# Expert slots of a mixture-of-experts layer: the moved x goes through a stage buffer to a dense matmul operand

## The chip, the core and the metric

The kernel runs on one core of a Trainium2 chip. Its time is the device time of one launch in microseconds (us); lower is better. Three runs of the kernel before gave a median of 1057.66 us, from 1057.39 to 1059.92.

## The reference

The kernel computes one transformer layer on x of shape 8 x 256 x 512 (2048 tokens of 512 floats), all in float32: cross attention to a context, then a mixture of experts. Only the second half matters here, with `h` the layer norm of the attention's result:

```python
logits = h @ gate_w.T                      # 32 experts
rw = softmax(logits); sel = top_k(sigmoid(logits), 4)
w = rw[sel] / rw[sel].sum()
cw_large[t, sel] += w                      # 32 large experts, inner width 192
cw_small[t, sel // 2] += w                 # 16 small experts, inner width 128
a = silu(h @ Wg[e]) * (h @ Wu[e]) * cw[:, e]
large = sum over e of a @ Wd[e]            # the same for small with cWg, cWu, cWd
x = x + large + 0.05 * small
```

## The kernel before, in words

Three stages follow one another, each a block of five instruction streams with a barrier between: `attention` (to 403 us), `route` (403 to 455 us) and `experts` (455 us to the end). Only the last has to do with most of the change.

`route` writes the normed tokens and the 32 weights of each to `xd` in DRAM, 544 floats a row (XW), and sorts the 8192 pairs of token and expert into slots of 128 tokens of one expert. There are at most 96 slots (NS); with these inputs 78 are run. Tables in SBUF tell of each slot: the token numbers (`tok`), the rows of the result (`dst`), the expert (`slot_e`) and which of four weight buffers it is in (`slot_buf`). A large expert and its small one are computed side by side, 192 + 128 = 320 columns (IW).

In `experts`, slot s uses buffers of parity p = s % 2, and its work goes through five queues:

- GpSimd, `gather(s)`: copies a column of `tok` to `idx`, and an indirect DMA brings the 128 rows to `xg`. `add(s)` adds the slot's y to the result by an indirect DMA that accumulates; each waits for the one before it.
- VectorE, `turn(s)`: transposes xg in blocks of 32 x 32 to `xb`, with a written step of four floats.
- ScalarE, `x_move(s)`: four DMAs move the 32-row quarters of xb so that each lands on all 128 partitions of `xT`. After all four, xT is x transposed, laid out [128, 128 tokens, 4]: the weight operand `xT[p][:, :, c]` of L1633 has a step of four floats.
- TensorE, `gate_up(s)`: 4 + 4 products of 128 x 128 with 320 columns, to `g_ps` and `u_ps`. In the profile each float32 product is two matmuls, so 8 and 8.
- ScalarE `silu(s)`, then VectorE `gated(s)`: a = silu(g) * u * the slot's weight column `wt`, which `weights_of` takes from xg by the expert's number.
- TensorE `transpose_a(s)` (three turns of a), VectorE `at_evac(s)` to `aT`, TensorE `down(s)`: 3 products (6 matmuls) of 512 columns to `y_ps`, ScalarE `y_evac(s)` to `yb`.

The order within a turn of the loop is written out by hand for each engine. For slot s: TensorE does transpose_a(s-1), gate_up(s), down(s-1). ScalarE does silu(s), x_move(s+2), y_evac(s-1). VectorE does at_evac(s-1), turn(s+2), gated(s), weights_of(s+2). GpSimd does add(s-1), gather(s+4). SyncE loads the next expert's weights into one of four buffers as slots are done. Slots 0 and 1 stand before the loop; a register loop over pairs of slots follows, with an `If` that skips the unused pairs up to NS. Each engine handles its instructions in order.

Of the kernel before, what the change touches and what calls it, by code (L numbers as in the profile page):

```python
# [5 lines left out]
ALU = mybir.AluOpType  # L6
ACT = mybir.ActivationFunctionType
AX = mybir.AxisListType
F32 = mybir.dt.float32
I32 = mybir.dt.int32  # L10
# [4 lines left out]
P = 128  # L15
# [972 lines left out]
def route(nc, gw, gw_loaded, xs, ident, new, xd, out, tabs, wts, W, w_loaded, kept, xd_stored):  # L988
# [5 lines left out]
    with ExitStack() as ctx:  # L994
# [130 lines left out]
        def _(act):  # L1125
# [42 lines left out]
            act.preload_act_table_set("natural_log_exp_and_others")  # L1168
# [135 lines left out]
        def _(dve):  # L1304
# [55 lines left out]
            dve.memset(tok[:, NS:NS + 4], 0)  # L1360
            dve.memset(slot_e[:, NS:NS + 4], 0)
            dve.memset(slot_buf[:, NS:NS + 4], 0)
# [64 lines left out]
def experts(nc, ident, xd, out, tabs, wts, W, w_loaded):  # L1427
# [4 lines left out]
    with ExitStack() as ctx:  # L1432
# [6 lines left out]
        xg = [sb(f"xg{i}", [P, XW], F32) for i in range(2)]  # L1439
        wt = [sb(f"wt{i}", [P, 2], F32) for i in range(2)]  # L1440
        xb = [sb(f"xb{i}", [P, D], F32) for i in range(2)]
        xT = [sb(f"xT{i}", [P, P, C], F32) for i in range(2)]
# [4 lines left out]

        g_ps = [ps(f"g_ps{i}", [P, 512]) for i in range(2)]
# [5 lines left out]
        turned, gu_full = sem("turned"), sem("gu_full")  # L1454
        x_ready = [sem(f"x_ready{i}") for i in range(2)]
        wt_ready = sem("wt_ready")
# [6 lines left out]
        def moved(s, p):  # L1463

            return (s - p) * (QB * DMA // 2) + QB * DMA
# [25 lines left out]
        @block.gpsimd  # L1491
        def _(pool):
            def gather(s, p):

                if not (isinstance(s, int) and s < 2):
                    pool.wait_ge(turned, s - 1)
                    pool.wait_ge(wt_ready, s - 1)
                pool.tensor_copy(idx[p][:, :], tok[:, bass.ds(s, 1)]).then_inc(idx_ready, 1)  # L1498
                pool.wait_ge(idx_ready, s + 1)
                pool.sem_inc(passed, 1)  # L1500
                pool.indirect_dma_start(xg[p][:, :], None, xd[:, :], bass.IndirectOffsetOnAxis(idx[p][:, :], 0))\  # L1501
                    .then_inc(x_loaded[p], DMA)

            def add(s, p):


                pool.tensor_copy(yidx[p][:, :], dst[:, bass.ds(s, 1)]).then_inc(yi_ready, 1)
                pool.wait_ge(yi_ready, s + 1)
                pool.sem_inc(passed, 1)
                pool.wait_ge(y_empty, s + 1)  # L1510
                pool.sem_inc(passed, 1)
                if not (isinstance(s, int) and s == 0):
                    pool.wait_ge(y_added, s * DMA)
                    pool.sem_inc(passed, 1)
                pool.indirect_dma_start(out[:, :], bass.IndirectOffsetOnAxis(yidx[p][:, :], 0), yb[p][:, :], None,  # L1515
                                        compute_op=ALU.add).then_inc(y_added, DMA)

            for s in range(4):
                gather(s, s % 2)
            gather(4, 0)  # L1520
            add(0, 0)
            gather(5, 1)
            n, last = count(pool)
            with pool.Fori(1, NS // 2) as i:
                with pool.If(i < n):
                    for p in range(2):
                        add(i * 2 + p - 1, 1 - p)
                        gather(i * 2 + p + 4, p)
            add(last + 1, 1)
            pool.wait_ge(y_added, last * DMA + 2 * DMA)  # L1530
            for p in range(2):
                pool.wait_ge(x_loaded[p], n * DMA + 2 * DMA)

        @block.scalar
        def _(act):
            def x_move(s, p):

                act.wait_ge(turned, s + 1)
                if not (isinstance(s, int) and s < 2):
                    act.wait_ge(gu_full, s - 1)  # L1540
                for i in range(QB):
                    act.dma_start(xT[p][:, i * Q:(i + 1) * Q, :].rearrange("m r c -> m (r c)"),  # L1542
                                  xb[p][i * Q:(i + 1) * Q, :]).then_inc(x_ready[p], DMA)
# [11 lines left out]
            def slot(s, p, first=False):  # L1555
                silu(s, p)
                x_move(s + 2, p)
                if not first:
                    y_evac(s - 1, 1 - p)

            x_move(0, 0)
            x_move(1, 1)
            slot(0, 0, first=True)
# [12 lines left out]
        def _(dve):  # L1576
# [4 lines left out]
            def weights_of(s, p):  # L1581

                e = dve.value_load(slot_e[0:1, bass.ds(s, 1)], min_val=0, max_val=E_ - 1)  # L1583
                dve.wait_ge(x_loaded[p], (s - p) * (DMA // 2) + DMA)
                if not (isinstance(s, int) and s < 2):
                    dve.wait_ge(a_ready, s - 1)
                dve.tensor_copy(wt[p][:, 0:1], xg[p][:, bass.ds(e + D, 1)]).then_inc(wt_ready, 1)
                dve.wait_ge(wt_ready, s + 1)
                dve.tensor_scalar(wt[p][:, 1:2], wt[p][:, 0:1], SMALL, None, ALU.mult)

            def turn(s, p):

                dve.wait_ge(x_loaded[p], (s - p) * (DMA // 2) + DMA)
                if not (isinstance(s, int) and s < 2):
                    dve.wait_ge(x_ready[p], moved(s - 2, p))
                dve.transpose(xb[p][:, :].rearrange("p (j r c) -> p j c r", r=Q, c=C), xg[p][:, 0:D]).then_inc(turned, 1)  # L1596
# [10 lines left out]
            for p in range(2):  # L1607
                turn(p, p)
                weights_of(p, p)
            turn(2, 0)  # L1610
            gated(0, 0)
            weights_of(2, 0)
            at_evac(0, 0)
            turn(3, 1)
            gated(1, 1)
            weights_of(3, 1)
            n, last = count(dve)
            with dve.Fori(1, NS // 2) as i:  # L1618
                with dve.If(i < n):  # L1619
                    for p in range(2):  # L1620
                        at_evac(i * 2 + p - 1, 1 - p)
                        turn(i * 2 + p + 2, p)
                        gated(i * 2 + p, p)
                        weights_of(i * 2 + p + 2, p)
# [3 lines left out]
        def _(pe):  # L1628
            def gate_up(s, p, buf):
                pe.wait_ge(x_ready[p], moved(s, p))  # L1630
                for ps_, g in ((g_ps, 0), (u_ps, 1)):
                    for c in range(C):
                        m = pe.matmul(ps_[p][:, 0:IW], xT[p][:, :, c],  # L1633
                                      W[:, bass.ds(buf, 1), (2 * c + g) * IW:(2 * c + g + 1) * IW]
                                      .rearrange("p a f -> p (a f)"),
                                      start=(c == 0), stop=(c == C - 1))
                m.then_inc(gu_full, 1)
# [26 lines left out]

            slot(0, 0, first=True)
# [6 lines left out]
            transpose_a(last + 1, 1)  # L1672
            down(last + 1, 1, pe.value_load(slot_buf[0:1, bass.ds(last + 1, 1)], min_val=0, max_val=NW - 1))


def build(nc, t, out):
    xd = nc.dram_tensor("xd", (NT * P, XW), F32, kind="Internal").ap()
    with ExitStack() as ctx:
# [6 lines left out]
        tabs = (sb("tok", [P, NS + 4], U32), sb("dst", [P, NS], U32), sb("slot_e", [P, NS + 4], I32),  # L1685
                sb("slot_buf", [P, NS + 4], I32), sb("cum_i", [P, E_], I32), sb("turns", [P, 2], I32))
# [50 lines left out]
```

## Time and profile before

| | |
|---|---|
| median of three runs | 1057.66 us |
| the profiled execution | 1061.51 us, its span 1059.8 us |
| TensorE busy | 986.3 us, 93% |
| VectorE, ScalarE, GpSimd busy | 49%, 30%, 28% |
| mean granted TensorE clock | 0.965 |
| HBM traffic | 123 GB/s over the span |

A row of a timeline gives the start in us from the span's beginning, the length in us, the engine, the line, the operation and its tiles, and in brackets the idle time before it and what ended it. PE is TensorE's matmul, PEld its weight load, DVE VectorE, ACT ScalarE, POOL GpSimd; a q behind a name means the queue of that engine, as for the issue of a DMA. Matmuls overlap, so the distance between starts is their cost, not their length.

### The profile page before, as it was taken

How to read it: one execution, taken by the hardware profiler on the slowest of the kernel's cores; microseconds unless marked ns; L12 is line 12 of the kernel's file. 1: busy time of each engine (PE TensorE's matmuls, PEld its weight loads, DVE VectorE, ACT ScalarE, POOL GpSimd, SP SyncE). 2: the span in 40 equal slices, each digit the busy share in tenths (PEclk: the TensorE clock that was granted, in tenths of full speed). 3: DMA queues.
4: the chain of work that ended last, by engine and by line, in shares of the span. 5: the costliest groups of instructions: out<-in, count | busy, mean ns of one | idle time of the engine just before them, and what ended most of it. 6: DMA issues, size and time to landing. Idle time of an engine off the chain costs nothing.

```text
span 1059.8 us, 18705 instructions
## 1 busy us (share of the span) xinstructions
PE 986.3 (93%) x5163; PEld 726.0 (69%) x5164; DVE 524.5 (49%) x1233; ACT 314.0 (30%) x631; POOL 300.3 (28%) x399
## 2 busy tenths in 40 slices
PE   7789999999999988449999999999999999999994
PEld 6557666676665535337878778777787777877872
DVE  4677677777677726933333333333333333333331
ACT  2245465555555535901111111111111111111110
POOL 3011101011120001223434344343443434434432
PEclk9999999999999989669999999999999999999997
DMA  6163234231431008227897998989888899889563
GB/s 208 45 166 77 66 91 102 86 86 56 121 80 51 32 31 304 105 72 174 219 244 181 249 253 219 243 218 254 199 221 215 211 259 249 213 208 251 111 114 68
DMA packets 102603, 168.23 MB, mean 159 GB/s; under 512 B 15520, under 2 KB 65824, under 8 KB 98208
## 3 DMA queue, kind: packets, MB, share of 16 engines
q1 hardware_dynamic: 36624, 103.11, 31.0%
q0 software_dynamic: 17792, 43.30, 21.6%
q10 hardware_dynamic: 48144, 21.25, 7.4%
q8 instruction: 27, 0.44, 0.2%
q14 instruction: 16, 0.13, 0.0%
HBM read 101.29 MB, written 29.36 MB: 123 GB/s over the span
## 4 chain that ended last, share of the span: by engine, by line
PE 54%; DMA 1%; issue 1%; DVEq 0%; DVE 0%; ACTq 0%; POOL 0%; ACT 0%; SPq 0%; POOLq 0%
PE y_ps L1650 19%; PE g_ps L1633 17%; PE u_ps L1633 16%; PE at_ps L1642 2%; DMA xg<-xd,gidx 0%; DMA xT<-xb 0%; ACTq L1542 0%; POOL out_x L1515 0%; DVEq L1618 0%; DVE xb L1596 0%; ACT sg L1547 0%; DVEq L1583 0%; ACT yb L1553 0%; DVE aT L1579 0%; DVEq L1619 0%
## 5 line engine op out<-in xcount | busy, mean ns | idle before, releaser
L1650 PE MATMUL y_ps<-W,aT 128*128 x468 | 216.3, 598 | 3.6 <-DVE aT L1579 3.6
L1633 PE MATMUL g_ps<-W,xT 128*128 x624 | 192.2, 451 | 13.3 <-DMA xT<-xb 13.0
L1515 POOL DMA_INDIRECT out_x<-yb,yidx x78 | 125.3, 1606 | 278.1 <-ACT yb L1553 194.4
L518 DVE TENSOR_REDUCE mx<-s 128x2 f32<-128x512 f32 x256 | 163.4, 682 | 59.3 <-PE s L709 58.6
L397 ACT ACTIVATE pt<-stp 128x512 f32<-128x512 f32 x256 | 139.1, 596 | 148.1 <-PE stp L723 147.4
L1633 PE MATMUL u_ps<-W,xT 128*128 x624 | 180.7, 432 | 0.0
L1633 PEld LDWEIGHTS g_ps<-W,xT 128*128 128x128 f32 x624 | 168.3, 311 | 15.2 <-issue 15.1
L1633 PEld LDWEIGHTS u_ps<-W,xT 128*128 128x128 f32 x624 | 171.0, 308 | 0.0
L1650 PEld LDWEIGHTS y_ps<-W,aT 128*128 128x128 f32 x468 | 89.6, 192 | 85.7 <-issue 79.6
L1596 DVE STREAM_TRANSPOSE xb<-xg 128x512 f32<-128x512 f32 x80 | 89.1, 1114 | 79.5 <-DMA xg<-xd,gidx 76.2
L1547 ACT ACTIVATE sg<-g_ps 128x320 f32<-128x320 f32 x78 | 34.2, 438 | 305.8 <-PE u_ps L1633 305.8
L1600 DVE SCALAR_TENSOR_TENSOR a<-u_ps,wt,sg 128x192 f32<-128x192 f32 x78 | 32.6, 418 | 183.8 <-ACT sg L1547 183.8
L1553 ACT COPY yb<-y_ps 128x512 f32<-128x512 f32 x78 | 45.7, 586 | 197.5 <-PE y_ps L1650 116.0
L1501 POOL DMA_INDIRECT xg<-xd,gidx x82 | 82.7, 1008 | 65.4 <-POOL gidx L1498 64.6
L709 PE MATMUL s<-kst,qst 96*128 96x256 bf16 x512 | 81.7, 275 | 10.5 <-DVE mx L518 9.8
L1579 DVE COPY aT<-at_ps 128x384 f32<-128x384 f32 x78 | 43.5, 558 | 87.9 <-PE at_ps L1642 82.9
L723 PE MATMUL stp<-qst,kst 98*128 98x256 bf16 x512 | 78.3, 276 | 4.0 <-DMA qst<-nm 4.0
L709 PEld LDWEIGHTS s<-kst,qst 96*128 96x128 bf16 x512 | 44.1, 98 | 51.2 <-DVE mx L518 24.1
L739 PE MATMUL ov<-pt,vx 128*32 128x256 f32 x1024 | 70.0, 392 | 1.9 <-ACT xo L381 1.8
L1498 POOL COPY gidx<-tok 128x1 uint32 (+1 forms) x82 | 60.0, 732 | 28.2 <-POOLq L994 17.2
L767 PE MATMUL side<-Wfc,oT 128*128 128x512 f32 x128 | 62.1, 601 | 1.5 <-ACT oT L387 1.5
L723 PEld LDWEIGHTS stp<-qst,kst 98*128 98x128 bf16 x512 | 49.5, 98 | 17.9 <-issue 5.6
(197 smaller groups left out, 842.9 us busy)
## 6 DMA issues: line engine op xcount, KB each, us to landing
W<-in_wts SPq DMA_DIRECT2D x32, 1280.0 KB
W<-in_wts SPq DMA_DIRECT2D x32, 768.0 KB
xT<-xb ACTq DMA_DIRECT2D x320, 64.0 KB
qst<-q SPq DMA_DIRECT2D x42, 256.0 KB, 5.0
xs<-in_x SPq DMA_DIRECT2D x8, 512.0 KB, 3.6
ctxT<-in_ctx SPq DMA_DIRECT2D x8, 512.0 KB, 4.0
out_x<-xs SPq DMA_DIRECT2D x16, 256.0 KB, 2.3
kst<-k SPq DMA_DIRECT2D x48, 64.0 KB, 2.1
```

The source lines that it names most:

```text
L397: act.activation(pt[g % 2][:, 2 * (j % 2) + r, :, :], stp[n % STP][:, :, :], ACT.Exp, scale=DH ** -0.5).then_inc(exp_done, 1)
L518: dve.tensor_reduce(mx[j // CH % 2][:, h:2 * G:G], s1[r][:, :, :], AX.X, ALU.max)\
L709: m = pe.matmul(s1[r][:, t, :], qst[b % 2][0:ROWS_QK, head(j, r), t * P:(t + 1) * P], kst[b % 2][0:ROWS_QK, head(j, r) // C, :], start=Tru ...
L723: m = pe.matmul(stp[n % STP][:, t, :], kst[b % 2][0:ROWS_ST, head(j, r) // C, t * P:(t + 1) * P], qst[b % 2][0:ROWS_ST, head(j, r), :], st ...
L739: m = pe.matmul(ov[c * VW:(c + 1) * VW, g % 2, :], vx[b % 2][:, t, g % 2 * C + c, :], pt[(b * G + g) % 2][:, c, t, :], start=(t == 0), sto ...
L767: m = pe.matmul(side[:, :], oT[t][:, c, :], Wfc[:, c, :], start=(c == 0), stop=(c == C - 1))
L1498: pool.tensor_copy(idx[p][:, :], tok[:, bass.ds(s, 1)]).then_inc(idx_ready, 1)
L1501: pool.indirect_dma_start(xg[p][:, :], None, xd[:, :], bass.IndirectOffsetOnAxis(idx[p][:, :], 0))\
L1515: pool.indirect_dma_start(out[:, :], bass.IndirectOffsetOnAxis(yidx[p][:, :], 0), yb[p][:, :], None, compute_op=ALU.add).then_inc(y_added, ...
L1596: dve.transpose(xb[p][:, :].rearrange("p (j r c) -> p j c r", r=Q, c=C), xg[p][:, 0:D]).then_inc(turned, 1)
L1633: m = pe.matmul(ps_[p][:, 0:IW], xT[p][:, :, c], W[:, bass.ds(buf, 1), (2 * c + g) * IW:(2 * c + g + 1) * IW] .rearrange("p a f -> p (a f) ...
L1650: m = pe.matmul(y_ps[:, :], aT[p][:, c, :], W[:, bass.ds(buf, 1), GW + c * D:GW + (c + 1) * D].rearrange("p a d -> p (a d)"), start=(c == ...
```

## The change

For slots from 1 on, the moved x lands in a new `stage` buffer, laid out [128, quarter, chunk, 32], and VectorE's new `place(s)` copies it to xT, which is now [128, chunk, 128 tokens]: the operand of a product is dense. The turn reads with a step of four floats and writes with none; the rows of the gate and up weights are ordered on the host to fit. The turn and the move run three slots ahead instead of two, the gather five instead of four. The weight column is taken in two steps: `weight_next` (to `wn`, with the turn) and `weight_now` (to `wt`).

The orders become: ScalarE x_move(s+3), silu(s), y_evac(s-1); VectorE at_evac(s-1), weight_now(s+1), place(s+1), turn(s+3), gated(s); GpSimd add(s-1), gather(s+5). TensorE's order stays.

Slot 0's x is transposed by TensorE from xg to `xt_ps` and copied to xT by ScalarE. Sixteen identity transposes run on TensorE ahead of it and sixteen ahead of the last down. The first four gathers index `tok` directly. `route` loses one preload of an activation table, and the tables get six spare columns instead of four.

```diff
-            act.preload_act_table_set("natural_log_exp_and_others")
...
-            dve.memset(tok[:, NS:NS + 4], 0)
-            dve.memset(slot_e[:, NS:NS + 4], 0)
-            dve.memset(slot_buf[:, NS:NS + 4], 0)
+            dve.memset(tok[:, NS:NS + 6], 0)
+            dve.memset(slot_e[:, NS:NS + 6], 0)
+            dve.memset(slot_buf[:, NS:NS + 6], 0)
...
+        wn = [sb(f"wn{i}", [P, 1], F32) for i in range(2)]
...
-        xT = [sb(f"xT{i}", [P, P, C], F32) for i in range(2)]
+        stage = [sb(f"stage{i}", [P, QB, C, Q], F32) for i in range(2)]
+        xT = [sb(f"xT{i}", [P, C, P], F32) for i in range(2)]
...
+        xt_ps = ps("xt_ps", [P, 512])
...
-        turned, gu_full = sem("turned"), sem("gu_full")
+        xt_full, x0_ready, turned, copied, gu_full = (sem(n) for n in ("xt_full2", "x0_ready", "turned", "copied",
+                                                                       "gu_full"))
...
-        wt_ready = sem("wt_ready")
+        wn_ready, wt_ready = sem("wn_ready"), sem("wt_ready")
...
-            return (s - p) * (QB * DMA // 2) + QB * DMA
+            return (s - p) * (QB * DMA // 2) + p * QB * DMA
...
             def gather(s, p):
...
+                if isinstance(s, int) and s == 2:
+                    pool.wait_ge(xt_full, 1)
+                elif not (isinstance(s, int) and s < 2):
+                    pool.wait_ge(turned, s - 2)
...
-                    pool.wait_ge(turned, s - 1)
-                    pool.wait_ge(wt_ready, s - 1)
-                pool.tensor_copy(idx[p][:, :], tok[:, bass.ds(s, 1)]).then_inc(idx_ready, 1)
-                pool.wait_ge(idx_ready, s + 1)
-                pool.sem_inc(passed, 1)
-                pool.indirect_dma_start(xg[p][:, :], None, xd[:, :], bass.IndirectOffsetOnAxis(idx[p][:, :], 0))\
+                    pool.wait_ge(wn_ready, s - 1)
+                if isinstance(s, int) and s < 4:
+                    rows = tok[:, s:s + 1]
+                else:
+                    pool.tensor_copy(idx[p][:, :], tok[:, bass.ds(s, 1)]).then_inc(idx_ready, 1)
+                    pool.wait_ge(idx_ready, s - 3)
+                    pool.sem_inc(passed, 1)
+                    rows = idx[p][:, :]
+                pool.indirect_dma_start(xg[p][:, :], None, xd[:, :], bass.IndirectOffsetOnAxis(rows, 0))\
...
             def add(s, p):
...
-            for s in range(4):
+            for s in range(6):
...
-            gather(4, 0)
...
-            gather(5, 1)
+            gather(6, 0)
...
                 with pool.If(i < n):
...
-                        gather(i * 2 + p + 4, p)
+                        gather(i * 2 + p + 5, 1 - p)
...
-                pool.wait_ge(x_loaded[p], n * DMA + 2 * DMA)
+                pool.wait_ge(x_loaded[p], n * DMA + (3 - p) * DMA)
...
             def x_move(s, p):
...
-                act.wait_ge(turned, s + 1)
-                if not (isinstance(s, int) and s < 2):
-                    act.wait_ge(gu_full, s - 1)
+                act.wait_ge(turned, s)
+                if not (isinstance(s, int) and s < 3):
+                    act.wait_ge(copied, s - 2)
...
-                    act.dma_start(xT[p][:, i * Q:(i + 1) * Q, :].rearrange("m r c -> m (r c)"),
+                    act.dma_start(stage[p][:, i, :, :].rearrange("m c r -> m (c r)"),
...
             def slot(s, p, first=False):
+                x_move(s + 3, 1 - p)
...
-                x_move(s + 2, p)
...
-            x_move(0, 0)
+            act.wait_ge(xt_full, 1)
+            act.copy(xT[0][:, :, :], xt_ps[:, :].rearrange("p (c t) -> p c t", c=C)).then_inc(x0_ready, 1)
             x_move(1, 1)
+            x_move(2, 0)
...
-            def weights_of(s, p):
+            def weight_next(s, p):
...
+                dve.tensor_copy(wn[p][:, :], xg[p][:, bass.ds(e + D, 1)]).then_inc(wn_ready, 1)
+            def weight_now(s, p):
+                dve.wait_ge(wn_ready, s + 1)
...
-                dve.tensor_copy(wt[p][:, 0:1], xg[p][:, bass.ds(e + D, 1)]).then_inc(wt_ready, 1)
+                dve.tensor_copy(wt[p][:, 0:1], wn[p][:, :])
+                dve.tensor_scalar(wt[p][:, 1:2], wn[p][:, :], SMALL, None, ALU.mult).then_inc(wt_ready, 1)
...
-                dve.tensor_scalar(wt[p][:, 1:2], wt[p][:, 0:1], SMALL, None, ALU.mult)
...
             def turn(s, p):
...
-                dve.wait_ge(x_loaded[p], (s - p) * (DMA // 2) + DMA)
+                weight_next(s, p)
+                if not (isinstance(s, int) and s < 3):
+                    dve.wait_ge(x_ready[p], moved(s - 2, p))
+                dve.transpose(xb[p][:, :], xg[p][:, 0:D].rearrange("t (c q j) -> t j c q", c=C, j=QB)).then_inc(turned, 1)
+            def place(s, p):
+                dve.wait_ge(x_ready[p], moved(s, p))
...
-                    dve.wait_ge(x_ready[p], moved(s - 2, p))
-                dve.transpose(xb[p][:, :].rearrange("p (j r c) -> p j c r", r=Q, c=C), xg[p][:, 0:D]).then_inc(turned, 1)
+                    dve.wait_ge(gu_full, s - 1)
+                dve.tensor_copy(xT[p][:, :, :].rearrange("m c (i r) -> m c i r", i=QB),
+                                stage[p][:, :, :, :].rearrange("m i c r -> m c i r")).then_inc(copied, 1)
...
             def gated(s, p):
...
-            for p in range(2):
-                turn(p, p)
-                weights_of(p, p)
+            weight_next(0, 0)
+            weight_now(0, 0)
+            turn(1, 1)
...
-            gated(0, 0)
-            weights_of(2, 0)
-            at_evac(0, 0)
-            turn(3, 1)
-            gated(1, 1)
-            weights_of(3, 1)
+            def slot(s, p, first=False):
+                if not first:
+                    at_evac(s - 1, 1 - p)
+                weight_now(s + 1, 1 - p)
+                place(s + 1, 1 - p)
+                turn(s + 3, 1 - p)
+                gated(s, p)
+            slot(0, 0, first=True)
+            slot(1, 1)
...
-                        at_evac(i * 2 + p - 1, 1 - p)
-                        turn(i * 2 + p + 2, p)
-                        gated(i * 2 + p, p)
-                        weights_of(i * 2 + p + 2, p)
+                        slot(i * 2 + p, p)
...
+            def transpose_x0():
+                pe.wait_ge(x_loaded[0], DMA)
+                for c in range(C):
+                    m = pe.transpose(xt_ps[:, c * P:(c + 1) * P], xg[0][:, c * P:(c + 1) * P], ident[:, :])
+                m.then_inc(xt_full, 1)
+            def keep_clock(n):
+                for _ in range(n):
+                    pe.transpose(xt_ps[:, 0:P], ident[:, :], ident[:, :])
             def gate_up(s, p, buf):
-                pe.wait_ge(x_ready[p], moved(s, p))
+                if isinstance(s, int) and s == 0:
+                    pe.wait_ge(x0_ready, 1)
+                else:
+                    pe.wait_ge(copied, s)
...
-                        m = pe.matmul(ps_[p][:, 0:IW], xT[p][:, :, c],
+                        m = pe.matmul(ps_[p][:, 0:IW], xT[p][:, c, :],
...
+            keep_clock(16)
+            transpose_x0()
...
+            keep_clock(16)
...
-        tabs = (sb("tok", [P, NS + 4], U32), sb("dst", [P, NS], U32), sb("slot_e", [P, NS + 4], I32),
-                sb("slot_buf", [P, NS + 4], I32), sb("cum_i", [P, E_], I32), sb("turns", [P, 2], I32))
+        tabs = (sb("tok", [P, NS + 6], U32), sb("dst", [P, NS], U32), sb("slot_e", [P, NS + 6], I32),
+                sb("slot_buf", [P, NS + 6], I32), sb("cum_i", [P, E_], I32), sb("turns", [P, 2], I32))
...
-        gu = np.stack([both("g"), both("u")], 2).reshape(E_, QB, C, Q, 2, IW).transpose(0, 3, 1, 2, 4, 5)
-        gu = gu.reshape(E_, P, GW)
+        gu = np.stack([both("g"), both("u")], 2).reshape(E_, C, P, 2, IW).transpose(0, 2, 1, 3, 4).reshape(E_, P, GW)
```

## Rows read from the trace of the kernel before

**Rows 1.** The page, part 4: shares of the span in the chain of waits, by line.
```profile
PE y_ps L1650 19%; PE g_ps L1633 17%; PE u_ps L1633 16%; PE at_ps L1642 2%; DMA xg<-xd,gidx 0%; DMA xT<-xb 0%; ACTq L1542 0%; POOL out_x L1515 0%; DVEq L1618 0%; DVE xb L1596 0%; ACT sg L1547 0%; DVEq L1583 0%; ACT yb L1553 0%; DVE aT L1579 0%; DVEq L1619 0%
```

**Rows 2.** Timeline of slot 32: start us, length us, engine, line, operation, tiles, [idle before].
```profile
701.90 0.49 PE L1642 MATMUL at_ps<-ident,a 128*128 128x128 f32 x3
...
702.23 2.44 PE L1633 MATMUL g_ps<-W,xT 128*128 x8
...
702.43 0.56 DVE L1579 COPY aT<-at_ps 128x384 f32<-128x384 f32 x1 [1.18 <-PE at_ps L1642]
...
704.32 1.11 DVE L1596 STREAM_TRANSPOSE xb<-xg 128x512 f32<-128x512 f32 x1 [1.34 <-DMA xg<-xd,gidx]
704.50 2.32 PE L1633 MATMUL u_ps<-W,xT 128*128 x8
...
706.65 2.74 PE L1650 MATMUL y_ps<-W,aT 128*128 x6
...
706.85 0.44 ACT L1547 ACTIVATE sg<-g_ps 128x320 f32<-128x320 f32 x1 [3.72 <-PE u_ps L1633]
706.99 2.52 ACTq L1542 DMA_DIRECT2D xT<-xb  x4
...
707.66 0.34 DVE L1602 SCALAR_TENSOR_TENSOR a<-u_ps,wt,sg 128x128 f32<-128x128 f32 x1
...
709.23 0.49 PE L1642 MATMUL at_ps<-ident,a 128*128 128x128 f32 x3
...
709.63 0.59 ACT L1553 COPY yb<-y_ps 128x512 f32<-128x512 f32 x1 [2.34 <-PE y_ps L1650]
```

**Rows 3.** Groups by form (busy us, mean ns | idle), two single lines (ns min/median/max).
```profile
L1633 PEld LDWEIGHTS g_ps<-W,xT 128*128 128x128 f32 x624 | 168.3, 311 | 15.2 <-issue 15.1
...
L1650 PEld LDWEIGHTS y_ps<-W,aT 128*128 128x128 f32 x468 | 89.6, 192 | 85.7 <-issue 79.6
L1596 DVE STREAM_TRANSPOSE xb<-xg 128x512 f32<-128x512 f32 x80 | 89.1, 1114 | 79.5 <-DMA xg<-xd,gidx 76.2 <-DMA xT<-xb 3.0
...
L1587 DVE COPY wt<-xg 128x1 f32 x80 | 12.3, 154 | 25.7 <-DVE a L1602 25.7
...
L1542 ACTq DMA_DIRECT2D xT<-xb x320: 550/626/1295, 461.4 to 1039.3; - x160
...
L1369 DVE TENSOR_SCALAR xl<-xs,mv_new,rstd_new x5: 543/545/548, 406.5 to 408.3; 128x512 f32<-128x512 f32 x5
```

**Rows 4.** Timeline of VectorE: three turns that waited for the gathered x.
```profile
498.54 1.11 DVE L1596 STREAM_TRANSPOSE xb<-xg 128x512 f32<-128x512 f32 x1 [1.18 <-DMA xg<-xd,gidx]
...
889.62 1.11 DVE L1596 STREAM_TRANSPOSE xb<-xg 128x512 f32<-128x512 f32 x1 [2.84 <-DMA xg<-xd,gidx]
...
1027.16 1.11 DVE L1596 STREAM_TRANSPOSE xb<-xg 128x512 f32<-128x512 f32 x1 [1.11 <-DMA xg<-xd,gidx]
```

**Rows 5.** Timeline of the expert stage's start; one window's busy times, clock, DMA.
```profile
460.31 1.08 DVE L1596 STREAM_TRANSPOSE xb<-xg 128x512 f32<-128x512 f32 x1 [4.60 <-DMA xg<-xd,gidx]
...
461.42 5.27 ACTq L1542 DMA_DIRECT2D xT<-xb  x8
...
466.64 4.17 PE L1633 MATMUL g_ps<-W,xT 128*128 x8 [12.97 <-DMA xT<-xb]
...
474.21 0.55 PE L1642 MATMUL at_ps<-ident,a 128*128 128x128 f32 x3 [1.24 <-DVE a L1602]
...
469.00:470.00 1.00, 1.00 (x3) 0.63 (x2) 0.00 (x0) 0.00 (x0) 0.00 (x0) 0.50 0.00 0
```

**Rows 6.** Timeline and window of the last down products (columns as above).
```profile
1045.02 5.48 PE L1650 MATMUL y_ps<-W,aT 128*128 x6 [3.60 <-DVE aT L1579]
...
1044.00:1050.00 6.00, 4.98 (x6) 1.85 (x6) 0.56 (x1) 0.00 (x0) 1.19 (x2) 0.50 0.41 85
```

**Rows 7.** Timeline of the router's first instructions on ScalarE and TensorE.
```profile
403.08 1.28 ACT L1168 ACT_TABLE_LOAD   x1 [5.63 <-PEq L50]
...
403.12 1.06 PE L1214 MATMUL r_xt<-ident,xs 128*128 128x128 f32 x8 [1.85 <-PEq L50]
```

## The prediction

> **What bounds the kernel now.** I read the chain of waits first. It lies on TensorE for 54% of the span, nearly all in the expert loop's down, gate and up products [rows 1]: the expert stage, 78 slots from 466.6 us, is bound by TensorE and by nothing else. The timeline of one slot shows why [rows 2]. I count time in a slot from T0, the start of the turn of the previous slot's `a` (701.90); the next slot begins at 709.23, so a slot is 7.33 us. Inside it the gate products begin at +0.33, the up products at +2.60, the down products at +4.75; TensorE never rests. Then I read the groups by form, for durations [rows 3]. The other engines have slack: `a` of the slot is ready at +6.10 (707.66 + 0.34), 1.2 us before TensorE asks for it.
>
> **Dense operand: a gain.** Gate begins 2.27 us before up, up 2.15 us before down, with eight matmuls each [rows 2]. The missing 0.12 us stands at the first gate weight load. A load of xT, read with a step of four floats, takes 311 ns, one of aT, dense, 192 ns [rows 3]. Behind a matmul of 269 ns (2.15/8) either hides; behind the short turns of `a` only the dense one does, and 311 - 192 = 0.12 us is just what is missing. So TensorE's own slot becomes 7.21 us: -0.12 x 77 = -9.2 us. Bounds: 0 (the gap is something else) to -9.2; I take all of it, since the two differences agree.
> The Trainium skill (TensorE: Matmul & The Clock Gate, LDWEIGHTS) has the load's time depend on the count of columns alone; by that a dense operand would change nothing, and this term would be 0. The two rows differ at the same 128 columns, and I go by them.
>
> **The order on ScalarE and VectorE: a loss.** Before, ScalarE does silu(s), issues the four moves of slot s+2, then copies y. Now it issues the moves of slot s+3 ahead of silu(s), and they wait for turn(s+3), which VectorE does in the same slot, after the copy of aT, weight_now and the new place. So silu is queued behind the turn and behind four DMA issues. In step:
> - the aT copy starts at +0.53 and ends at +1.09 [rows 2]; the two small weight instructions (154 ns each [rows 3], overlapping) and the wait for them: +1.35;
> - place, 128x512 floats from SBUF to SBUF, is not in the trace. Lower bound the 154 ns of a one-column copy, upper the 1.11 us of the stream transpose, which moves as many floats with a step; nearest is the 545 ns of the unit-step tensor_scalar [rows 3], which I take: +1.9. Beside it VectorE's queue reads the expert number for the weight column. Its cost shows in the idle before the old weight copies, 25.7 us in 78, 0.33 each behind an instruction that it partly overlaps [rows 3]; with the small copy the turn starts at +2.30;
> - the turn, 1.11 us: it wrote with a step of four floats and now reads with one. Bounds 0.55 (if only the written step cost) to 1.11; I keep 1.11: +3.41;
> - four issues on ScalarE's queue: 2.52 us (706.99 to 709.51), and they do hold ScalarE: the y copy follows at 709.63, 0.12 after the last [rows 2]. So silu at 3.41 + 0.03 + 2.52 + 0.12 = +6.08, against +4.95 before;
> - silu to the end of `a` takes 1.15 us (706.85 to 708.00 [rows 2]), and 0.06 to TensorE: +7.29.
> That is later than 7.21, so the loop VectorE, ScalarE, VectorE becomes the bound: +0.075 x 76 = +5.7 us. The floor is then 7.29, almost the old 7.33, and has no slack left for anything late.
> The Trainium skill (DMA: Bandwidth & Descriptors, Issuing engines are not separate DMA queues) calls the sequencer's time to issue a DMA usually small beside the DMA. By it moving four issues ahead of silu would be nearly free; the rows show 2.52 us a slot. It is weighed as the first rival.
>
> Two things are late. (1) The gathered x. The turn of the old kernel waited 76.2 us in 72 slots for it, 2.84 us at most (889.62) [rows 3, 4]. Counting its start from T0, the mean is +2.03. The gather keeps its lead of two slots between issue and turn; it is issued some 0.2 us earlier in the slot, as the y copy no longer stands behind the issues, but the slot is 0.12 shorter, and the weight copy now goes before the turn (+0.27). So every slot whose turn began after +2.11 delays the loop: 31 of 76, the first at 498.54 and the last at 1027.16 [rows 4], on average 0.23 us over all 76: 17 us. A stall postpones TensorE, not the gathers of the next two slots, so it is repaid in part: carried slot by slot over the 76 starts, 8.3 us stay. (2) The issues: four take 2.52 us in most slots, but single ones up to 1.3 us instead of 0.63 [rows 3]; the mean of four is 2.62, 0.10 x 76 = 7.9 us, that before fell into slack. Both together, carried slot by slot and partly covering one another: +12.8 us. Bounds 0 to 17 + 8 = 25.
> Steady stage: -9.2 + 5.7 + 12.8 = +9.3 us.
>
> **The start.** Before: the first turn at 460.31, eight issues to 466.69, gate at 466.64, slot 1's T0 at 474.21; the gate products began at the lower clock, 0.50 [rows 5], 4.17 us instead of 2.27. Now slot 0 is turned by TensorE: gather 0.3 us earlier without the index copy, landed at 460.0, four transposes and ScalarE's copy, gate at 461.4 and done by 466. But nothing follows from it: silu(0) stands behind the moves of slots 1, 2 and 3. The chain: turn(1) ends 462.75, its issues 465.4, landed 467.8 (as before, 2.4 after the issue), place(1) 468.4, turn(3) 470.4, issues of slot 3 to 473.0, the table load 1.28 us [rows 7], silu 0.44, `a` 0.7: T0 at 475.6, +1.4 us. TensorE has then been idle some 9 us, so slot 1 starts at the lower clock, as slot 0 did: six matmuls at twice 0.267 us, +1.6. Start: +3.0; bounds -3 (silu not held up) to +6 (all of slot 1 slow). The 16 identity transposes ahead cost nothing, they run while the gather is in flight.
>
> **The end.** The last down runs 5.48 us at clock 0.50 [rows 6], against 2.74 in a slot [rows 2], after 3.6 us with only three transposes since 1040. Sixteen transposes, at the 0.11 us of those of `a` some 1.8 us, now fill that idle time while VectorE and the aT copy are awaited, so they delay nothing. I take it that the clock stays up: -2.6. Bounds 0 and -2.7.
>
> **The table load in the router.** 1.28 us at 403.08; the first four of TensorE's eight transposes beside it need half of 1.06 us, and ScalarE's copy of them then waits for the table [rows 7]. If the set from attention still serves, ScalarE starts 0.6 us earlier and the router's chain, which goes through it, keeps that: -0.6. Bounds -1.3 and +1.3 (the load returns ahead of Ln). Longer tables (six zeros for four), the xt_ps bank and the other row order of the gate weights on the host: 0.
>
> **Sum.** +9.3 + 3.0 - 2.6 - 0.6 = +9.1 us. The profiled execution took 1061.5 us, 1.7 more than its span of 1059.8; on it the sum gives 1070.6. It lay 3.8 above the median of three, 1057.7. From the median: 1066.8.
>
> **Rivals.**
> - The issues don't hold up silu (or the turn comes so early that it doesn't matter): then TensorE stays the bound, the steady stage gives -9.2, the start about +1, with the end and the router -11.4: 1046. For it: TensorE had 1.2 us of slack at `a`. Against: the y copy's start 0.12 after the last issue. This is the case on the other side; it decides once the loop of +7.29 with all its lateness lies under 7.21. Chance 0.13.
> - The turn reads with a step more cheaply than it wrote (0.55 us): floor 6.7, only the latest gathers and issues stall, +6.5 of them, steady -2.7, total -2.9: 1055. Chance 0.15.
> - Place costs like the transpose, 1.11 us (interleaved runs of 32 floats): the turn starts at +2.6, each slot 0.3 later, less cover for lateness: steady +29.5, total +29: 1087. Chance 0.15.
> - The dense load doesn't shorten the slot (the change doesn't do what it says): TensorE's slot stays 7.33, and lateness beyond it adds 12.9: 1070. Chance 0.07.
> - The forecast: 0.50.
>
> **How the numbers follow.** A difference under 0.3% (3.2 us) can't be told from none here. Faster: the first rival and a third of the second, 0.18. Same: the rest of the second and 0.07 of the forecast's lower edge, 0.17. Slower: 0.65. The range 1050 to 1084 takes in the second and fourth rivals and most of the way to the third; the forecast's own is 1060 to 1074.
>
> **What would show it.** In the new timeline: x_move's issues ahead of silu, silu at about +6.1 instead of +4.95, TensorE idle before most turns of `a` with VectorE's `a` named as what ended it, slots of 7.3 to 9 us. Gate and up equally long (2.15 us), gate's weight load 190 ns. Place 0.55 us. First gate near 461.4, then TensorE idle to 475. Last down in 2.7 us. If silu still starts at +4.9, the forecast is wrong at the queue; if slots are a uniform 7.21, wrong altogether.

## The result and the profile after

The changed kernel takes 1085.8 us (median of four, 1083.58 to 1088.92); the kernel before takes 1057.53 us (median of four, 1054.99 to 1059.92). The ratio is 1.0266 [1.0238, 1.0294]: slower by 28.3 us, where 9.1 was forecast (1066.8, range 1050 to 1084). The sign was right, the size was not, and the time lies outside the range.

I cut both profiled executions at the same points: the router's first transpose, VectorE's memset of `a` that opens the expert stage, and T0 of the slots 1, 2 and 77 (T0: start of the turn of the previous slot's `a`).

| stretch (us) | before | after | difference | forecast |
|---|---|---|---|---|
| attention stage | 403.12 | 399.53 | -3.6 | 0 |
| router and tables | 52.41 | 50.71 | -1.7 | -0.6 |
| expert stage to T0 of slot 1 | 18.68 | 18.83 | +0.15 | +1.4 |
| slot 1 | 7.41 | 9.23 | +1.8 | +1.6 |
| the 75 slots from T0 of slot 2 | 550.68 (7.342 each) | 578.12 (7.708) | +27.4 | +9.3 |
| T0 of slot 77 to the end | 27.48 | 25.40 | -2.1 | -2.6 |
| span | 1059.8 | 1081.8 | +22.0 | +9.1 |

The attention stage has no edit, and in the executions of this study, all with the same code there, it took 397.3 to 403.1 us: that row is spread. It is also why the spans differ by 22.0 and the medians by 28.3: the profiled execution of before (1061.51) lies above its timed runs, that of after (1083.58) is the lowest of four. All that matters is in the steady slots.

The chain of waits of the changed kernel (shares of the span by line), the line that answers to [rows 1]:
```profile
ACTq L1551 10%; PE y_ps L1690 10%; PE g_ps L1673 8%; PE u_ps L1673 8%; PE at_ps L1682 4%; DVE xb L1612 4%; DVEq L1594 2%; ACT sg L1556 2%; DVE a L1626 1%; DVE a L1624 1%; DVE wt L1603 0%; DVE wn L1596 0%; DMA xg<-xd,tok 0%; DVE xT L1619 0%; PE xt_ps L1664 0%
```
L1551 is the issue of x's moves on ScalarE's queue. It was 0% of the chain and is now its largest item; the three product lines fell from 52% to 26%. The bound went from TensorE to a loop through VectorE and ScalarE's queue.

The timeline of slot 14, T0 = 570.39, beside [rows 2]; its first rows are the end of slot 13:
```profile
566.61 2.54 ACTq L1551 DMA_DIRECT2D stage<-xb  x4
...
569.19 0.44 ACT L1556 ACTIVATE sg<-g_ps 128x320 f32<-128x320 f32 x1 [5.57 <-issue]
...
570.39 0.55 PE L1682 MATMUL at_ps<-ident,a 128*128 128x128 f32 x3
...
570.57 7.78 SPq L985 DMA_DIRECT2D W<-in_wts  x2
...
570.78 2.34 PE L1673 MATMUL g_ps<-W,xT 128*128 x8
570.98 0.56 DVE L1590 COPY aT<-at_ps 128x384 f32<-128x384 f32 x1 [0.64 <-PE at_ps L1682]
571.45 0.14 DVE L1603 COPY wt<-wn 128x1 f32<-128x1 f32 x1
...
571.86 0.43 DVE L1619 COPY xT<-stage 128x512 f32<-128x512 f32 x1 [0.20 <-DVE wt L1604]
...
572.80 0.15 DVE L1596 COPY wn<-xg 128x1 f32 x1 [0.51 <-issue]
572.87 1.09 DVE L1612 STREAM_TRANSPOSE xb<-xg 128x512 f32<-128x512 f32 x1
572.95 2.32 PE L1673 MATMUL u_ps<-W,xT 128*128 x8
...
574.07 3.17 ACTq L1551 DMA_DIRECT2D stage<-xb  x4
...
575.11 2.74 PE L1690 MATMUL y_ps<-W,aT 128*128 x6
...
577.29 0.44 ACT L1556 ACTIVATE sg<-g_ps 128x320 f32<-128x320 f32 x1 [6.21 <-issue]
...
578.09 0.34 DVE L1626 SCALAR_TENSOR_TENSOR a<-u_ps,wt,sg 128x128 f32<-128x128 f32 x1
...
578.49 0.55 PE L1682 MATMUL at_ps<-ident,a 128*128 128x128 f32 x3 [0.64 <-DVE a L1626]
```
The four issues (574.07 to 577.24) stand ahead of silu, which starts 0.05 later, and TensorE waits 0.64 us for `a`. "issue" behind sg means that nothing but ScalarE's own queue held it. The rows also show two kinds of slots: four issues of 2.54 us give one of 7.46, four of 3.17 one of 8.10. In [rows 2] the issues began at +5.09, behind silu; here they begin at +3.68.

Single lines (ns, min/median/max), against [rows 3]:
```profile
L1551 ACTq DMA_DIRECT2D stage<-xb x320: 550/627/1375, 457.3 to 1062.0; - x160
```
```profile
L1673 PEld LDWEIGHTS g_ps<-W,xT x624: 186/190/338, 456.5 to 1058.4; 128*128 128x128 f32 x156
```
```profile
L1619 DVE COPY xT<-stage x78: 426/427/512, 462.1 to 1057.9; 128x512 f32<-128x512 f32 x78
```
The median issue is what it was, but 34 of the 80 sets of four hold one over 0.7 us, 30 times the second of the four, mostly near 1.1 us; in the steady slots four take 2.79 us on average, against 2.62 before. The weight load fell from 311 to 190 ns. Place, not in the trace before, takes 427 ns.

Two windows of the issues (us, busy of PE, PEld, DVE, ACT, POOL, granted clock, DMA share, GB/s), of slot 13 and of slot 14:
```profile
566.60:569.20 2.60, 2.60 (x9) 1.49 (x8) 0.00 (x0) 0.01 (x1) 1.21 (x2) 1.00 0.99 131
574.10:577.30 3.20, 3.20 (x11) 1.64 (x9) 0.00 (x0) 0.01 (x1) 1.21 (x2) 1.00 1.07 298
```
In the long slot the DMA engines move 298 GB/s, most of it the expert's weights, whose load SyncE issued from 570.57; in the short one 131. The 75 steady slots fall into groups by this. In 28 the first and larger piece of a load (1280 KB) was issued 3.5 to 3.8 us before the first of the four issues: they take 7.90 us or more. In 28 it was the second piece (768 KB), 3.9 us or more before: 7.43 to 7.72 us. In 19 none was issued in the last 11 us: 7.465 us on average. This is a coincidence of rows until a run takes the load away.

The waits (engine line <- released by: us, times, longest):
```profile
ACT sg L1556 <- issue: 459.9, 76, 6.8
...
PEld at_ps L1682 <- DVE a L1626: 88.3, 76, 7.1
```
TensorE now waits 88.3 us for `a`. VectorE's wait for the gathered x, 76.2 us in [rows 3], is down to 1.5 us in 3 turns; what gives the gathers more time is worked out below.

### The profile page after: what moved, and what is told of

It is laid out like the page before. It is cut to its first block, busy times and chain, and to the rows that moved or that the text cites. A ratio compares the mean times of both kernels' runs of the same rounds, so it can differ in the third digit from the quotient of the medians.

```text
span 1081.8 us, 18895 instructions
## 1 busy us (share of the span) xinstructions
PE 996.1 (92%) x5199; PEld 623.6 (58%) x5200; DVE 549.3 (51%) x1390; ACT 312.6 (29%) x631; POOL 304.3 (28%) x397
## 4 chain that ended last, share of the span: by engine, by line
PE 31%; ACTq 10%; DVE 7%; issue 4%; DVEq 3%; ACT 2%; DMA 1%; POOL 0%; POOLq 0%
ACTq L1551 10%; PE y_ps L1690 10%; PE g_ps L1673 8%; PE u_ps L1673 8%; PE at_ps L1682 4%; DVE xb L1612 4%; DVEq L1594 2%; ACT sg L1556 2%; DVE a L1626 1%; DVE a L1624 1%; DVE wt L1603 0%; DVE wn L1596 0%; DMA xg<-xd,tok 0%; DVE xT L1619 0%; PE xt_ps L1664 0%
## 5 line engine op out<-in xcount | busy, mean ns | idle before, releaser
L1525 POOL DMA_INDIRECT out_x<-yb,yidx x78 | 128.8, 1651 | 305.7 <-ACT yb L1562 238.8
L1673 PE MATMUL g_ps<-W,xT 128*128 x624 | 185.8, 441 | 0.9 <-ACT xT L1571 0.9
L1673 PEld LDWEIGHTS u_ps<-W,xT 128*128 128x128 f32 x624 | 118.6, 190 | 49.4
L1673 PEld LDWEIGHTS g_ps<-W,xT 128*128 128x128 f32 x624 | 114.0, 193 | 39.9 <-issue 3.4
L1511 POOL DMA_INDIRECT xg<-xd,gidx x79 | 79.6, 1007 | 64.3 <-POOL gidx L1507 62.1
L1682 PEld LDWEIGHTS at_ps<-ident,a 128*128 128x128 f32 x234 | 24.5, 141 | 91.6 <-DVE a L1626 88.3
L1682 PE MATMUL at_ps<-ident,a 128*128 128x128 f32 x234 | 43.0, 293 | 27.8 <-DVE a L1626 25.0
```

The source lines that it names most:

```text
L1673: m = pe.matmul(ps_[p][:, 0:IW], xT[p][:, c, :], W[:, bass.ds(buf, 1), (2 * c + g) * IW:(2 * c + g + 1) * IW] .rearrange("p a f -> p (a f) ...
L1682: m = pe.transpose(at_ps[:, c, :], a[p][:, c * P:(c + 1) * P], ident[:, :])
```

## The experiments

My theory: the change is slower because silu stands behind the turn and the moves' issues, and the loop through both queues is longer than TensorE's slot. The rival: the staged and copied operand itself costs (the copy, the stage, a longer VectorE program), wherever the moves stand. For the rest of the miss, the weight loads were the suspect behind the long issues, and the read of the expert's number behind the late turn. All runs had the kernel before on the same chip, 1057.5 to 1059.6 us.

**silu_first.** ScalarE's order alone:
```
                silu(s, p)
+               x_move(s + 3, 1 - p)
                if not first:
                    y_evac(s - 1, 1 - p)
```


> The changed kernel with one order undone: ScalarE does silu(s), x_move(s+3), y_evac(s-1) instead of x_move(s+3), silu(s), y_evac(s-1). Theory A (silu queued behind the turn and four DMA issues makes the loop through VectorE and ScalarE the bound): slots fall from 7.73 us on average to TensorE's own 7.21 us, 0.52 x 75 = 39 us less; the first silu stands behind 8 issues instead of 12, about 2.6 us less at the start; the y copy goes back behind the issues, at no cost. About 1044 us (1040 to 1050), faster than the kernel before. Theory B (VectorE's added copy, or the stage buffer and its DMAs, slow the slots wherever silu stands): slots stay above 7.5 us, 1075 us or more. Theory C (A, but a dense operand gives nothing): slots of 7.33 us, about 1053 us.


Measured: 1043.72 us (1041.55 to 1047.04), ratio 0.9853 [0.9831, 0.9875]. One line's place is worth 42 us against the changed kernel. Slots are 7.21 us, mean 7.238. Its waits:
```profile
ACT sg L1556 <- PE u_ps L1673: 276.2, 74, 7.0
...
DVE wn L1596 <- DMA xg<-xd,gidx: 61.5, 58, 5.5
```
silu is released by the up product again, at +4.84, and `a` is ready at +5.98, which leaves 1.2 us of slack. The rival falls: stage, place and turn are all still there. The waits for the gather are back at 61.5 us, nearly all in that slack; one slot of 9.1 us, behind the wait of 5.5, is the exception. It is slot 56, which is long in other runs too (9.9 us in lead_two, 8.1 in best, 7.6 with small loads); why it is stays open.

**silu_first_step4.** The same, with the operand back at its step of four floats:
```
-        xT = [sb(f"xT{i}", [P, C, P], F32) for i in range(2)]
+        xT = [sb(f"xT{i}", [P, P, C], F32) for i in range(2)]
...
-    pe.matmul(ps_[p][:, 0:IW], xT[p][:, c, :],
+    pe.matmul(ps_[p][:, 0:IW], xT[p][:, :, c],
```


> As the kernel with silu first, but xT laid out as before the change, with a step of four floats in the weight operand; place writes it so, which may make that copy 1.1 us instead of 0.43. Theory A with the dense operand worth 0.12 us a slot: gate weight load 309 ns, gate to up 2.27 us, slots 7.33 us, 0.12 x 77 = 9 us slower than the kernel with silu first. Rival (the load's length hangs on its columns alone, the 0.12 us is something else): no difference between the two, within 2 us.


Measured: 1051.22 us (1049.09 to 1054.29), ratio 0.9934 [0.991, 0.9957]. Its weight load and its place:
```profile
L1673 PEld LDWEIGHTS g_ps<-W,xT x624: 307/309/333, 459.1 to 1027.0; 128*128 128x128 f32 x156
...
L1619 DVE COPY xT<-stage x78: 634/639/645, 464.2 to 1026.4; 128x512 f32<-128x512 f32 x78
```
The usual slot is 7.33 us. The dense operand gives 0.12 us in the usual slot, as forecast (the medians are 7.5 us apart, where 9 was expected), and this is the whole gain of the staging: without it the other edits leave the slot where it was.

**lead_two.** x_move(s+2) stands ahead of silu(s), and the move of slot 2 ahead of the loop is dropped: four issues in front of silu still, but of a turn done a slot earlier.
```
-                x_move(s + 3, 1 - p)
+                x_move(s + 2, p)
                 silu(s, p)
```


> The changed kernel, ScalarE's order kept (moves ahead of silu), but the move is that of slot s+2, whose turn was done in the slot before, so its four issues need not wait for this slot's turn and run from about +0.7 to +3.4 us, before the up products end at +4.8. Theory A in its full form (what costs is the turn and the issues in one chain ahead of silu): silu back at +4.9, slots 7.21 us, about 1044 us. Rival D (issues ahead of silu cost 2.5 us wherever they begin): slots as in the changed kernel, 1083 us. If single issues become long here too, they have slack and the time does not show it.


Measured: 1044.77 us (1042.33 to 1045.1), ratio 0.9871 [0.9853, 0.9889]; usual slots of 7.21, the issues from about +0.7 to +3.3. Behind them silu is released by the up product again:
```profile
ACT sg L1556 <- PE u_ps L1672: 296.4, 73, 7.4
```
So issues ahead of silu cost nothing as such. What costs is that they wait for a turn of the same slot. That narrows the theory to the loop turn, issues, silu, `a`.

**no_keep.** Both `keep_clock(16)` left out.


> The changed kernel without both groups of sixteen identity transposes. In the trace: the last down products at the lower clock throughout, 5.5 us instead of 3.6, so the end 1.9 us longer. At the start gate of slot 0 begins at the same time at the lower clock, but T0 of slot 1 hangs on the issues and the first silu and does not move. In all 2 us more, which one run can't tell by its time; the rows can.


Measured, one run: 1082.37 us. From T0 of slot 77 to the end 26.07 us against 25.40; T0 of slot 1 lies 18.88 us behind the stage's start against 18.83. Its last down product:
```profile
1067.06 4.40 PE L1690 MATMUL y_ps<-W,aT 128*128 x6 [2.51 <-DVE aT L1590]
```
With the transposes it takes 3.57 us, before the change 5.48 [rows 6]. By these two executions they are worth 0.7 us at the end and nothing at the start.

**small_loads.** SyncE's loads inside the loop fetch 32 columns per piece, at the same places and with the same waits. What this kernel leaves out is the rest of the weights of every expert after the first four, so most slots are computed with those of the first four experts; the shapes and the counts of all other operations stay:
```
-    load_piece(sp, wts, W, w_loaded, i, p, 0)
+    load_some(i, p, 0)      # W[:, p, 0:32] alone
...
-    load_piece(sp, wts, W, w_loaded, i, p, 1)
+    load_some(i, p, 32)     # W[:, p, 32:64] alone
```


> The changed kernel, but in the expert loop SyncE brings 32 columns of an expert's weights in each of the two pieces instead of the whole 2 MB (so most experts are computed with the first four experts' weights); all waits and orders stay. In the changed kernel four issues on ScalarE's queue take 2.52 us in about half of the slots and 3.0 to 3.8 in the other half; the long ones are those where a weight load was issued 4.1 us before and its bytes are in flight. Theory A2 (the load in flight makes the issues long): four issues take 2.5 us in every slot, all slots 7.46 us instead of 7.73 on average, 0.26 x 75 = 19 us less: about 1066 us. Rival E (GpSimd's indirect DMAs, or x's own moves, make them long): the mixture of 7.46 and 8.0 stays, 1085 us.


Measured: 1065.43 us (1064.69 to 1069.86), ratio 1.0082 [1.0054, 1.0109]. Its issues:
```profile
L1555 ACTq DMA_DIRECT2D stage<-xb x320: 550/625/741, 457.9 to 1044.6; - x160
```
No issue is over 0.75 us, four take 2.54, and nearly every slot is 7.46 us. The mean falls from 7.708 to 7.465, by 0.24 us, and so does that of four issues, from 2.79 to 2.54: 0.243 x 75 = 18.2 us is what the weight loads add to the changed kernel through ScalarE's issues. The coincidence of the windows is a cause.

**early_read.** VectorE's queue reads the expert's number at the start of the slot instead of between place and turn:
```
             def slot(s, p, first=False):
+                e = expert_of(s + 3)
                 ...
-                turn(s + 3, 1 - p)
+                turn(s + 3, 1 - p, e)
```


> The changed kernel with one step moved on VectorE's queue: the read of the expert number for turn(s+3) stands at the slot's beginning, ahead of the aT copy, where the queue waits anyway, instead of behind place. In the changed kernel VectorE is idle 0.5 us between place and the weight column. Theory A3 (that read holds the turn): the turn begins at +2.0 instead of +2.5, silu 0.5 us earlier, short slots fall from 7.46 to TensorE's 7.21, long ones from 8.0 to 7.5; the mean by the periods of the changed kernel's trace is 7.35, 0.36 x 75 = 27 us less: about 1059 us, as the kernel before. Rival F (the 0.5 us is the wait for place's own result or for the gathered x): no change, 1085 us.


Measured: 1064.56 us (1061.08 to 1070.38), ratio 1.0058 [1.0034, 1.0083]. The read is worth 0.27 us a slot (7.708 to 7.435), but I expected 7.35. The weight column is now copied at +1.81 instead of +2.41; yet 39 of 80 sets hold an issue over 0.7 us, four take 2.81 us on average, and the gathers are late again:
```profile
DVE wn L1597 <- DMA xg<-xd,gidx: 10.5, 17, 1.4
```
That left a question: do the long issues and the late gathers have one cause, or is the gather a bound of its own?

**early_small.** early_read and small_loads together, with the same weights left out.


> Both edits together: the expert number read early and the small weight loads (so again most experts are computed with the first four experts' weights). With the early read alone the slots took 7.45 us on average where 7.35 was expected: issues long in 38 of 80 moves, and VectorE waiting for the gathered x in 17 slots, 10.5 us in all. Theory G (both, the long issues and the late gathers, come from the weight load in flight): every slot at TensorE's 7.21, about 1046 us. Rival H (the gathers are late by GpSimd's own chain of adds): slots of 7.3 on average with VectorE waiting for x as before, 1052 us or more.


Measured: 1048.77 us (1048.01 to 1049.5), ratio 0.9895 [0.9876, 0.9914]; usual slots of 7.21, and of the waits for the gather this is left:
```profile
DVE wn L1601 <- DMA xg<-xd,gidx: 2.3, 5, 0.8
```
With the loads small, the long issues are gone (none over 0.684 us) and so are most of the waits for x: the weight load in flight causes the first and most of the second (theory G). And with the changed kernel's own order on ScalarE the loop now fits under TensorE's 7.21.

**router_only.** The kernel before without the preload of the table in the router.


> The kernel before without the table preload at the router's start, nothing else. By the forecast's step 0.6 us less; by the changed kernel's trace, in which no table load stands in the router, up to 1.2 us less; if the load comes back ahead of Ln, 0 to 1.3 us more. The medians can't tell this, the length of the router stage in the trace can: it is 52.4 us in the kernel before, from its first instruction at 403.07 to the first of the expert stage at 455.47.


Measured: 1056.93 us (1055.1 to 1060.45), ratio 0.9998 [0.9977, 1.0019]. The stretch of the router took 50.70 us against 52.41, but this stretch is 50.7 in some executions and 51.8 in others of the same code without the preload, only one execution with it was profiled, and the whole shows no difference that can be measured.

**best.** silu first, the early read, and at the start silu and `gated` of slot 0 ahead of the moves of slots 2 and 3, with the table of silu loaded beside the first gate product:
```
+            act.preload_act_table_set("silu_and_others")
             x_move(1, 1)
+            silu(0, 0)
             x_move(2, 0)
-            slot(0, 0, first=True)
+            x_move(3, 1)
```


> The changed kernel with silu first, the early read of the expert number, and at the start silu and the gating of slot 0 ahead of the moves of slots 2 and 3, with the silu table loaded while ScalarE waits for x. Theory A: slots 7.21 us as with silu first; slot 1's T0 about 4 us earlier (one group of four issues, 2.6, and the table load, 1.3), and slot 1 no longer at the lower clock, 1.4 us less: 5 us less than with silu first, about 1039 us. If T0 of slot 1 then hangs on place(1) and its landing, 1041.


Measured: 1040.55 us (1039.04 to 1043.47), ratio 0.9842 [0.9811, 0.9874]. It beats both kernels, by 17 and by 45 us. The start:
```profile
456.89 1.28 ACT L1572 ACT_TABLE_LOAD   x1
...
462.03 0.44 ACT L1556 ACTIVATE sg<-g_ps 128x320 f32<-128x320 f32 x1 [3.86 <-PE u_ps L1680]
462.04 5.70 ACTq L1551 DMA_DIRECT2D stage<-xb  x8
...
463.32 0.55 PE L1689 MATMUL at_ps<-ident,a 128*128 128x128 f32 x3 [1.33 <-DVE a L1629]
```
T0 of slot 1 comes 11.93 us after the stage's start, not 18.83, and slot 1 takes 7.61. Over silu_first, with 14.99 and 8.64, that is 4.1 us; the medians differ by 3.2.

## Why the forecast had the sign right and the size wrong

**Dense operand, -9.2: right.** 0.12 us in the usual slot, from silu_first against silu_first_step4. One reading on the way was not sound: a load of 311 ns is longer than the 269 ns of the matmul behind which it was said to hide. It does hide, since up begins 2.15 us before down in both traces, but not by being shorter. The Trainium skill (TensorE: Matmul & The Clock Gate, LDWEIGHTS) has the load's time depend on the columns alone; 309 and 190 ns for the same 128 columns contradict it here.

**The loop as the bound: right in kind, 0.17 us a slot too short.** The forecast was 7.29, the floor is 7.465 (small_loads). Step by step: the aT copy ended at +1.15 (+1.09 forecast), and place ended at +1.90, as forecast, starting 0.11 later and running 427 ns, not 545. Then came the first error. I had priced the read of the expert's number by idle time of 0.33 us, partly covered, and put the turn at +2.30. It leaves VectorE idle for 0.51 us, and the turn started at +2.48. The second is small: the issues begin 0.11 us after the turn, not 0.03. The turn itself (1.09), four undisturbed issues (2.54) and silu to `a` (1.14) were right. In part this was made good: silu starts 0.05 us after the last issue, not 0.12. So the floor brings, with the dense operand, (7.465 - 7.342) x 75 = +9.2 us, where the forecast had 5.7 - 9.2 = -3.5. This is the largest miss, 12.7 us: a loop rightly drawn, whose terms for the register read and for the way from the turn to the issues were too small.

**Lateness, +12.8: 5.4 too little, and both its parts wrong.** This is the second step that failed, and the one whose reasoning was wrong. I took the long issues at 0.10 us a slot from the trace before, where the issues begin at +5.09. Moved to +3.68 they meet the weight load, which is in flight then, and the second of the four waits: 0.243 a slot, 18.2 us and not 7.9. The gathers, priced at 8.3 after repayment, cost nothing: VectorE waited 1.5 us in 3 turns. The lead of two slots that I gave a gather between issue and turn is wrong too. GpSimd runs behind, and the traces show 4.6 us from issue to turn before, waits included, and 6.0 in the changed kernel. About 0.4 us of the difference is the longer slot, 0.4 the later turn (+2.48 against a mean of +2.03) and 0.6 the earlier issue of the gather (a mean of +4.18 against +4.80, where I had 0.2 earlier). The gather itself is no faster: its last packet ends 4.1 us after its issue on average in both traces. No run took these three apart. So the steady stage is 9.2 + 18.2 = +27.4, against -3.5 + 12.8 = +9.3. Of the miss of 18.1 us there, 12.7 is the floor and 5.4 the lateness.

That a DMA's issue is dear was right: had it been small, as the Trainium skill (DMA: Bandwidth & Descriptors, Issuing engines are not separate DMA queues) says it usually is beside the DMA, the first rival would have held; the traces show 2.54 us a slot with the weight loads cut down and 2.79 with the whole ones. The third rival's 1087 lies near the result, but its mechanism (place of 1.11 us) did not occur. The second (a turn of 0.55) did not either, nor the fourth.

**The start, +3.0: +2.0.** TensorE turned slot 0's x, and its gate began 6.3 us after the stage's start, but nothing followed from it. Twelve issues hold ScalarE from 457.32, then the table load, and TensorE idles:
```profile
456.49 3.86 PE L1673 MATMUL g_ps<-W,xT 128*128 x8 [0.87 <-ACT xT L1571]
...
457.32 9.21 ACTq L1551 DMA_DIRECT2D stage<-xb  x12
...
466.56 1.28 ACT L1556 ACT_TABLE_LOAD   x1 [10.32 <-issue]
467.86 0.44 ACT L1556 ACTIVATE sg<-g_ps 128x320 f32<-128x320 f32 x1
...
469.06 0.90 PE L1682 MATMUL at_ps<-ident,a 128*128 128x128 f32 x3 [6.56 <-DVE a L1626]
...
469.75 3.97 PE L1673 MATMUL g_ps<-W,xT 128*128 x8
```
After 6.56 us idle the gate products of slot 1 take 3.97 us at a granted clock of 0.50, as those of slot 0 did before (4.17, [rows 5]), and slot 1 costs +1.8 (forecast +1.6). The chain to its T0 came out 1.25 us shorter than I had it. `best`, with the table loaded early and silu(0) ahead of the moves of slots 2 and 3, reaches that T0 6.9 us sooner: that is what the head start was worth.

**The end, -2.6: -2.1, partly for another reason.** The last down product took 3.57 us, not 2.74: the granted clock is 0.67 in the window of the transposes and 0.82 in that of the product (0.50 in [rows 6]):
```profile
1066.00:1069.00 3.00, 3.00 (x20) 2.75 (x19) 0.56 (x1) 0.00 (x0) 2.20 (x3) 0.67 0.47 46
1069.00:1073.00 4.00, 3.48 (x7) 1.32 (x6) 0.00 (x0) 0.40 (x1) 0.35 (x2) 0.82 0.47 103
```
Only 0.7 us of the gain goes with the transposes (no_keep). They took 2.85 us, not the 1.8 of the forecast, but the down product began as soon after the last turn of `a` as without them (3.08 and 3.06 us). Of the other 1.4 us, 1.1 is the down product: 4.40 us in no_keep behind 2.51 us of idle time, 5.48 before behind 3.60. Nothing was tried there.

**The router, -0.6:** router_only can't tell it from nothing.

**Still open:** why an issue waits when it does. Its place among the four isn't the reason: in the changed kernel 31 of the 40 steady issues over 0.8 us are the second, and 25 of the 40 begin 4.0 to 4.2 us after a piece of a load was issued; in early_read, where all four begin earlier, 27 of 47 are the third, and 26 begin 3.8 to 4.2 us after. But in lead_two the long ones begin 1.0 to 3.3 us after, so it isn't that time alone either; and in the changed kernel the time goes with the size of the piece. No run tried the load at another place of the slot.

## What to carry to other kernels

An operation on an engine's queue has a place and a partner: before an issue of DMAs is moved, read what the DMA engines and the queues do at the new place, since its old duration holds only for the old one. When the moved work waits for something of the same step, walk the whole loop through both queues, with the register reads in it, and compare it with the bound in hundredths of a microsecond; here 0.12 us gained and 0.5 us lost hung on that. If a loop does not fit, put what it feeds later behind what is due now: the same instructions gave 1043.7 or 1085.8 us.

## What the runs showed of the hardware that I had not expected

- Issuing DMAs can slow down while a large load is in flight: four issues of 64 KB each take 2.54 us at 131 GB/s and 3.17 at 298, single ones up to 1.375 us; with the loads cut down none is over 0.741.
- The same load makes indirect gathers late: VectorE's waits of 10.5 us (early_read) fell to 2.3 (early_small), and the last packet of a gather ends 3.7 us after its issue on average and 4.7 at most, where it was 4.15 and 6.3.
- A float32 weight load of 128 columns takes 309 ns with a step of four floats and 190 dense; a VectorE copy of 128x512 floats that writes with this step 639 ns, dense 427; ScalarE's copy of the same size from PSUM 1056 and 580. The stream transpose takes 1.11 us writing with the step and 1.09 reading with one.
- Reading a number from SBUF into a register on VectorE's queue leaves that engine idle for 0.51 us; issued at the slot's start, behind nothing that is due, that goes.
